# Two quads of heads in one PV bank, K two beats later, second-layer weights turned in beats 1 to 4

## The reference, cut to what matters

```python
x = L0_attn_x                                      # (8, 512, 128) fp32
x = x + attn(layernorm(x))                         # 16 heads of 8
x = x + ffn(layernorm(x))                          # 8 experts, 2 of them for each token

def attn(x):
    Q, K, V = proj(Wq, bq), proj(Wk, bk), proj(Wv, bv)      # (B, 16, 512, 8)
    scores = einsum('bhqd,bhkd->bhqk', Q, K) / sqrt(8)
    attn = softmax(scores)
    out = einsum('bhqk,bhkd->bhqd', attn, V)
    return out.reshape(B, S, D) @ Wo.T + bo

def ffn(t):
    top_v, top_i = top_k(t @ Wr.T + br, 2)                  # router
    h = relu(einsum('bsd,efd->bsef', t, W1) + b1)           # 512 hidden
    o = einsum('bsef,edf->bsed', h, W2) + b2
    return layer_norm(t + sum_over_the_two(o * weight))     # gamma, beta
```

## Time and profile before

| | |
|---|---|
| median of 3 runs | 753.96 us (751.37 to 755.16) |
| profiled execution | 752.29 us, its span 750.5 us |
| busy share of the span | PE 81%, DVE 65%, ACT 60%, POOL 32% |
| scores of T = 0 begin | 33.8 us |
| batches 0 to 7 begin | 33.8, 82.3, 133.6, 193.1, 254.2, 316.1, 377.7, 439.6 us |
| last scores end | 496 us |
| experts' part | about 548 us to the end |

### The profile page before, as it was taken

How to read it: one execution, slowest core, us unless ns; L and a number is a source line. 1 busy time by engine, 2 the same in 40 slices (tenths; PEclk the granted TensorE clock), 3 DMA queues, 4 the chain that set the end, 5 groups by cost and what they waited for, 6 DMA issues and landing times. The chain is left out here.

```text
span 750.5 us, 13269 instructions
## 1 busy us (share of the span) xinstructions
PE 609.3 (81%) x3750; PEld 321.2 (43%) x3750; DVE 489.0 (65%) x1319; ACT 447.4 (60%) x945; POOL 242.6 (32%) x454
## 2 busy tenths in 40 slices
PE   2899999879988997987987998995229998999680
PEld 1633333323333432332332333332128988888530
DVE  3579989968967985985995887751204444444357
ACT  2718888867956965875885786683114444544333
POOL 5200101150240332214115005016425665555534
PEclk9959999989998998998998899899559999999976
DMA  7552122122122122022112211000121221221193
GB/s 219 195 153 66 44 69 83 49 67 74 37 85 72 33 84 84 26 65 89 49 47 70 65 45 48 6 0 30 50 83 54 65 66 56 69 66 57 47 238 98
DMA packets 54216, 54.47 MB, mean 73 GB/s; under 512 B 8286, under 2 KB 37514, under 8 KB 54164
## 3 DMA queue, kind: packets, MB, share of 16 engines
q1 hardware_dynamic: 48372, 44.19, 20.8%
q0 software_dynamic: 4416, 8.53, 3.2%
q10 hardware_dynamic: 1376, 1.13, 0.5%
HBM read 29.01 MB, written 24.81 MB: 72 GB/s over the span
## 5 line engine op out<-in xcount | busy, mean ns | idle before, releaser
L643 DVE TENSOR_REDUCE mneg<-s_psum 128x1 f32<-128x512 f32 x512 | 325.9, 684 | 89.5 <-PE s_psum L810 55.7
L546 ACT ACTIVATE pt<-st_psum 128x512 f32<-128x512 f32 x512 | 279.9, 598 | 93.3 <-PE st_psum L826 82.7
L826 PE MATMUL st_psum<-qs,ks 64*128 64x512 f32 x512 | 202.5, 471 | 24.8 <-ACT pt L546 19.4
L810 PE MATMUL s_psum<-ks,qs 64*128 64x512 f32 x512 | 208.3, 482 | 3.3 <-DVE mneg L643 2.1
L896 PE MATMUL pv_psum<-pt,vst 128*16 128x512 f32 x1024 | 142.8, 632 | 0.0
L810 PEld LDWEIGHTS s_psum<-ks,qs 64*128 64x128 f32 x512 | 84.4, 196 | 120.2 <-DVE mneg L643 94.9
L826 PEld LDWEIGHTS st_psum<-qs,ks 64*128 64x128 f32 x512 | 82.4, 193 | 69.1 <-ACT pt L546 52.7
L1099 ACT ACTIVATE hid<-h_psum,b1c 128x256 f32<-128x256 f32 x144 | 57.2, 474 | 71.2 <-PE h_psum L1204 69.3
L1062 POOL DMA_INDIRECT results<-res,goal_now x72 | 71.6, 994 | 33.7 <-issue 33.7
L1211 PE MATMUL y_psum<-w2t,hid 128*128 128x128 f32 x576 | 73.1, 280 | 0.0
L1211 PEld LDWEIGHTS y_psum<-w2t,hid 128*128 128x128 f32 x576 | 68.9, 194 | 0.9 <-issue 0.2
(11 more groups left out here) (164 smaller groups left out, 711.3 us busy)
## 6 DMA issues: line engine op xcount, KB each, us to landing
parts<-high SPq DMA_DIRECT2D x32, 256.0 KB, 3.0
ks<-parts SPq DMA_DIRECT2D x128, 48.0 KB
qs<-parts SPq DMA_DIRECT2D x128, 48.0 KB
lot<-sent SPq DMA_DIRECT2D x37, 132.0 KB
parts<-low SPq DMA_DIRECT2D x16, 256.0 KB, 3.1
got<-results SPq DMA_DIRECT2D x16, 256.0 KB, 5.1
xres<-in_L_attn_x_dram SPq DMA_DIRECT2D x8, 256.0 KB, 3.6
pt<-in_L_ffn_W_dram SPq DMA_DIRECT2D x1, 2048.0 KB, 14.5
```

The costliest lines, as they stand in the source:

```text
L546: nc.scalar.activation(pt[:, n % PT_SLOTS, (g + 2) % 4, :], st_psum[:, k % ST_BANKS, :], ACT.Exp, scale=SCALE).then_inc(exp_done, 1)
L643: nc.vector.tensor_reduce(mneg[:, (n // 4) % 2, at:at + 1], s_psum[:, k % S_BANKS, :], AX_X, ALU.max, negate=True).then_inc(max_done, 1)
L810: mm(s_psum[:, k % S_BANKS, :], qs[rows, c, P * (n % 4):P * (n % 4) + P], ks[rows, c, g, :], start=True, stop=True).then_inc(s_made, 1)
L826: mm(st_psum[:, k % ST_BANKS, :], ks[rows, c, g, P * (n % 4):P * (n % 4) + P], qs[rows, c, :], start=True, stop=True).then_inc(st_made, 1)
```

## The change

Four edits, in `attention` only.

1. Two quads share the PV bank. Head g of an even quad keeps rows 32g to 32g+15, head g of the odd quad behind it takes rows 32g+16 to 32g+31. A matmul of L896 now has 32 columns of weights instead of 16, of which the 16 of the other quad are zeros, and the bank accumulates over 8 beats. `vst` becomes twice as large. The heads are numbered anew by `head_of`, so that 8 neighbouring heads come out together.
2. The copy of the bank is made in beats 0 and 8, and TURN is in beats 1 and 9; each treats 8 heads. The number of 128x128 transposes, 4 for a TURN, stays.
3. K moves from beat 3 to beat 5 (its store in SP's list with it).
4. The second layer's weights are turned in T = 1 to 4 instead of T = -4 to -1.

```diff
+def per_pair(T, offset):
+    m, r = divmod(T - offset, 8)
+    return m if r == 0 and 0 <= m < QUADS * B // 2 else None
+
+def head_of(c, g):
+    return 8 * (c // 2) + 2 * g + c % 2
...
-    if (q := per_quad(T, 13)) is not None:
-        yield "TURN", q
-    for kind, offset in (("XT", -14), ("K", -13), ("Q", -10), ("V", 7), ("OT", 26), ("O", 27), ("X2T", 30),
+    if (m := per_pair(T, 17)) is not None:
+        yield "TURN", m
+    for kind, offset in (("XT", -14), ("K", -11), ("Q", -10), ("V", 7), ("OT", 26), ("O", 27), ("X2T", 30),
...
 def expert_weights(T):
-    return range(2 * (T + 8), 2 * (T + 8) + 2) if -8 <= T < 0 else ()
+    if -8 <= T < -4:
+        return range(2 * (T + 8), 2 * (T + 8) + 2)
+    return range(E + 2 * (T - 1), E + 2 * (T - 1) + 2) if 1 <= T < 5 else ()
...
-        vst = sb("vst", [P, 2, TILES, H, 16])
+        vst = sb("vst", [P, 2, TILES, H // 2, 64])
...
-                if (b := once(T, -13)) is not None:
+                if (b := once(T, -11)) is not None:
                     store_parts(0, b)
...
-                if (q := per_quad(T, 12)) is not None:
-                    act.wait_ge(pv_made, 4 * q + 4)
+                if (m := per_pair(T, 16)) is not None:
+                    act.wait_ge(pv_made, 8 * m + 8)
...
-                if n % 4 == 0 and q > 0:
-                    pe.wait_ge(pv_copied, q)
+                if n % 8 == 0 and n > 0:
+                    pe.wait_ge(pv_copied, n // 8)
...
                 for g in range(4):
-                    ins = mm(pv_psum[32 * g:32 * g + 16, 0, :], vst[:, b % 2, n % 4, 4 * (q % QUADS) + g, :],
-                             pt[:, n % PT_SLOTS, g, :], start=(n % 4 == 0), stop=(n % 4 == 3))
+                    at = 16 * (q % 2)
+                    ins = mm(pv_psum[32 * g:32 * g + 32, 0, :],
+                             vst[:, b % 2, n % 4, 4 * (q % QUADS // 2) + g, at:at + 32],
+                             pt[:, n % PT_SLOTS, g, :], start=(n % 8 == 0), stop=(n % 8 == 7))
```

More of the change, by code:

```diff
@@ L186, in attention @@
         onorm = sb("onorm", [P, TILES, D])
-        rden = sb("rden", [P, TILES, 4])
+        rden = sb("rden", [P, TILES, 8])
         mneg = sb("mneg", [P, 2, TILES * 4])
@@ L338, in load_parts @@
                     dst = ks[rows, c, g] if w == 0 else qs[rows, c]
-                    sp.dma_start(dst.bitcast(F32), parts[b % 2, w, 4 * c + g]).then_inc(kq_in[c], 16)
+                    sp.dma_start(dst.bitcast(F32), parts[b % 2, w, head_of(c, g)]).then_inc(kq_in[c], 16)
             def beat(T):
@@ L399, in _ @@
             pool.wait_ge(pool_consts, 4)
-            nc.gpsimd.memset(vst[:, :, :, :, HD:HD + 1], 1.0).then_inc(pool_consts, 1)
+            nc.gpsimd.memset(vst[:].rearrange("p z j h (a r) -> p (z j h a) r", r=32)[:, :, HD:HD + 1], 1.0).then_inc(pool_consts, 1)
             nc.gpsimd.memset(tail[:], 0.0).then_inc(tail_ready, 1)
@@ L524, in take_side @@
                         act.wait_ge(pv_made, GROUPS * (of - 1))
-                    nc.scalar.copy(vst[:, of % 2, :, :, 0:HD],
-                                   side_psum[:, 0, :].rearrange("p (j h d) -> p j h d", j=TILES, d=HD))\
+                    nc.scalar.copy(vst[:, of % 2].rearrange("p j h (a r) -> p (j h a) r", r=32)[:, :, 0:HD],
+                                   side_psum[:, 0, :].rearrange("p (x d) -> p x d", d=HD))\
                         .then_inc(side_done, 1)
@@ L532, in beat @@
             def beat(T):
-                if (q := per_quad(T, 12)) is not None:
-                    act.wait_ge(pv_made, 4 * q + 4)
-                    if q >= 1:
-                        act.wait_ge(side_made, SIDE["TURN", q - 1] + 1)
+                if (m := per_pair(T, 16)) is not None:
+                    act.wait_ge(pv_made, 8 * m + 8)
+                    if m >= 1:
+                        act.wait_ge(side_made, SIDE["TURN", m - 1] + 1)
                     nc.scalar.copy(pvs[:], pv_psum[:, 0, :]).then_inc(pv_copied, 1)
@@ L653, in take_early @@
                 elif kind == "TURN":
-                    c = of % QUADS
+                    at = 8 * (of % 2)
                     dve.wait_ge(side_made, SIDE["TURN", of] + 1)
-                    sums = side_psum[:, 0, :].rearrange("p (j g r) -> p j g r", j=TILES, g=4)
+                    sums = side_psum[:, 0, :].rearrange("p (j h r) -> p j h r", j=TILES, h=8)
                     nc.vector.reciprocal(rden[:], sums[:, :, :, HD]).then_inc(rden_done, 1)
@@ L659, in take_early @@
                     nc.vector.tensor_tensor(
-                        onorm[:].rearrange("p j (h d) -> p j h d", d=HD)[:, :, 4 * c:4 * c + 4, :],
-                        sums[:, :, :, 0:HD], rden[:].unsqueeze(3).to_broadcast([P, TILES, 4, HD]),
+                        onorm[:].rearrange("p j (h d) -> p j h d", d=HD)[:, :, at:at + 8, :],
+                        sums[:, :, :, 0:HD], rden[:].unsqueeze(3).to_broadcast([P, TILES, 8, HD]),
                         ALU.mult).then_inc(side_done, 1)
```

## The result

The changed kernel takes 754.94 us (median of 20 executions, 751.17 to 756.77). The kernel before, run beside it, takes 751.88 us (20 executions, 748.38 to 755.19). The ratio is 1.0039, with a 95% interval of 1.0024 to 1.0054: 3 us slower, clear of the noise. Forecast were 741 us and a range of 732 to 750. The profiled execution of the changed kernel took 755.91 us, 754.2 of them in the span.

A forecast was written before the change was run, and what follows sets the result against it. TensorE was taken as nearest to full, DVE close behind, with time lost to stands and slow clock; -4.0 - 1.8 - 6.3 - 1.6 + 1.8 = -11.9 from 752.3 gave 740.4, forecast as 741 us, range 732 to 750.

The forecast's parts named there:

- The start: Second layer's weight transposes leave the way to the first scores: -4.0 us, 2.3 certain and 1.7 chosen, bounds -6.5 and +1.9.
- 1.05 us each at full clock: Ends of T = 1 to 4: eight moved transposes a beat, covered by DVE; at half clock 4.2 us more at worst.
- a fuller TensorE should be slow for less of the 17.1 us: T = 0 to 7: with the moved transposes TensorE would spend less than 17.1 us at 1.2 GHz.
- My lower bound of the gain, +1.9: Start, worst case: 2.3 us gained by the earlier first maximum, 4.2 lost to transposes at half clock.
- Start lost: Rival at the start: moved transposes run at half clock and give back all of the 4.0, 745 us; chance 0.06.
- The change touches neither the scatter nor the work of beats 7 and 8: Beats 7 and 8, where TensorE and DVE stand behind the scatter: left as they are, 0 us.
- scatter stand grows: Rival at beat 8: K's three stores start inside the scatter, 4.2 us more in six scatters, 766 us; chance 0.06.
- TURN of eight heads: Beat 1, where DVE has the router's work: 0.1 us allowed for the longer TURN, inside each -0.35.
- K in beat 5: Beats 3 to 6 take 14.01 us instead of 14.45 at full clock: -0.35 each, five times, -1.8 us.
- The clock behind beat 3: Beats 4 and 5 return to full clock once beat 3's stand is gone: 1.57 us four times, -6.3; bounds 0 and -6.3.
- clock not regained: Rival: beat 3's stand goes, but TensorE still idles and slow stretches fall elsewhere, 747 us; chance 0.20.
- the load's 14 ns: Values with 32 columns: one load's 14 ns more a beat over 128 beats, +1.8 us; bounds 0 and +14.7.

The follow-up runs named there:

- second pair of profiles: The kernel before and the changed kernel run once more, with stands, on another chip: 751.41 us and 754.03 us, ratio 1.0027.
- split start: Changed kernel with four second-layer weight blocks turned ahead of T = 0, four in T = 0 and 1, repeated transposes in T = 2 to 5: 745.23 us, 0.9918.
- filled start: Changed kernel with edit 4 undone and eight unread transposes repeated behind each of beats T = 0 to 5: 747.95 us, 0.9949; the split start also has repeated transposes.
- spread scatter: Kernel before with each scatter's eight transfers issued two a beat in beats 6 to 9: 712.69 us, 1.0003, without stands; three repeats 0.9996, 1.0016, 1.0000.
- the zeros alone: Kernel before with 16 columns of zeros beside the 16 of values, nothing else changed: 711.93 us, 0.9997, and 712.82 us, 1.0002, without stands.

## Why the prediction was wrong

**The start: the step that failed, -4.0 forecast, +6.65 measured (+4.05 in the second pair of profiles).** That the first scores and the first maximum come earlier was right: 4.4 and 3.3 us. Two assumptions behind it were not. The first was that the moved transposes cost "1.05 us each at full clock", with 4.2 us more "at worst". They ran at half clock. T = 1 to 4 take 18.4 us in place of 13.1, each of them above the 3.5 us that I had named as a sign of being wrong. Nor would DVE have covered them wholly at full clock: with the split start, T = 1 takes 2.73 us with eight transposes and was 2.39 before. The second, and the worse one, was that "a fuller TensorE should be slow for less of the 17.1 us". It was slow for 37.5, and T = 5 to 8, which have no moved work, take 18.8 us in place of 13.9. My lower bound of the gain, +1.9, had priced the transposes at half clock and had left all other work at the clock of before; this is why the measurement lies outside it. "Start lost" was the right rival by its mechanism, had a chance of 0.06, and its 745 us were too low for the same reason.

That this edit costs time is shown by the runs without stands: edit 4 alone is slower, 1.0047 (1.0028 to 1.0066), with T = 0 to 7 at 34.09 us. All but edit 4 was 0.9900 and all of it 0.9930, which points the same way, but in two groups and with intervals that overlap. How much longer the half clock lasts by edit 4 is less clear: 27.3 us with edit 4 alone, 17.1 to 27.3 in kernels without it, 37.5 with all four edits in each of three profiles. What in edits 1 to 3 adds the last 10 us beside edit 4 is open; by themselves they have 27.3. Of the +6.65, 2.6 us (6.65 less 4.05) are luck, since the first profile of the kernel before had its short stretch. That it is the clock is shown with stands: filling TensorE's idle time there removed the half clock and made T = 0 to 7 of the kernel without edit 4 23.65 us long, and 23.66 us with half of its transposes in T = 0 and 1. What made the clock fall the rows show only as an order of events. In the changed kernel TensorE stood for 0.79 us, worked for 0.72, stood for 1.66, and the clock was at 1.2 GHz from 31.8 on, at its next matmuls; with edit 4 alone it stood for 2.08 us and fell at 33.4. Before, the 4.20 us of transposes lay directly ahead of the first scores, and it fell at 38.6. I had read these transposes as work in the way of the scores. By the order of the rows they may also be what kept the clock up until there; that is argued and wasn't tried by itself.

On the Trainium skill's rule, "TensorE: Matmul & The Clock Gate", PE-mode transpose, that transposes don't count as busy, I had written that the trace disagrees. The rule's outcome, moved transposes at half clock, is what came. The runs don't bear out the rule as the Trainium skill puts it either: eight transposes behind each beat held 1.00 through T = 0 to 5 once the clock was high, and ahead of the scores, with transposes alone, they had sped up. That the same eight behind beats at 1.2 GHz did not bring it back in T = 1 to 4 would fit the rule. Which property of the work decides is open.

**The scatter: "The change touches neither the scatter nor the work of beats 7 and 8", 0 forecast, +4.9 measured.** With stands, beats 6 to 9 of batches 2 to 7 take 19.46 and 19.43 us on average in the two profiles of the kernel before, and 20.39 and 20.26 in the two of the changed one, of which 0.16 is Q's wait in beat 6. Counted from the start of the scatter, the maxima of beat 8 begin 8.7 to 11.7 us later before, and 11.4 to 11.9 us later in each of the 24 scatters of the changed kernel and of the two with the filled start. So the rival "scatter stand grows" was right in its sign, small in its size (0.8 us a scatter, 0.7 in the second pair, where it needed 2.8 to decide alone), and its reason is not the only one: batch 7 has no K to store and grows most, from 8.7 to 11.6. Edit 4 isn't the cause, since the filled start without it shows 11.6 to 11.8. Which of edits 1 to 3 it is stays open, because the runs that separate them fell in groups without stands. What the stand is stays open too. With it beats 6 to 9 of the changed kernel take 20.3 us on average in batches 2 to 7, without it 12.9, for the same code and the same 9.9 us of scatter on POOL.

**TURN of eight heads: 0.1 allowed, 0.23 measured.** XT in beat 2 and OT in beat 10 wait for it. The timeline of the changed kernel in T = 34:

```profile
146.11 0.35 DVE L670 RECIPROCAL rden<-side_psum 128x32 f32<-128x32 f32 x1
146.50 0.42 DVE L672 TENSOR_TENSOR onorm<-side_psum,rden 128x256 f32<-128x256 f32 x1
147.03 0.42 PEld L869 LDWEIGHTS side_psum<-ident,xn 128*128 128x128 f32 x4 [0.36 <-DVE onorm L672]
```

The groups by line give a mean of 348 ns for the reciprocal and 424 ns for the division, against 248 and 291 before: 0.23 us more in a row, and TensorE's weight load of XT waits 0.36 us for the end of it. The longer beats 2 and 10, 3.25 and 3.22 us for 3.01 and 2.99, are this. I had looked at beat 1, where TURN is issued, and not at beat 2, whose first side task stands behind it, and had forgotten beat 10. It cost 3.1 us, 2.7 in the second pair of profiles; without stands the two beats have the same lengths, 3.25 and 3.22.

**What was right.** K in beat 5: beat 3 without the wait for `low`, 14.0 us for beats 3 to 6. The clock behind beat 3: no drop there in any of the changed kernel's five batches, in any group, while it drops in all five of the group of edit 4 alone (4.71 us for beat 4). So the rival "clock not regained" is out. Beat 13, the load's 14 ns, and copies at nothing were right as well; for the loads +1.8 was taken, and the zeros alone show about 1. My 0.9 ns a column holds only as the price of one more column: it would make 14 ns of a whole load of 16, which takes 95.

**The sum.** Against the profiled execution of before, -11.9 was forecast. The start adds 10.65 to it, the scatter 4.9, beats 2 and 10 add 3.1, and the smaller differences of the table take 3.05 off again: +3.7, the difference of the spans. In the second pair of profiles, with the start of the kernel before at its longer length, the spans differ by 0.8 us.

**A better version.** Edits 1 to 3 with the split and filled start: 0.9918 with stands, and with the spread scatter 0.9811 and 0.9818 without.

## What to carry to other kernels

Work that stands in the way of the critical engine may be what holds its clock (here that is argued, not shown): before moving it, read the granted clock behind the place it leaves, and price everything up to the next change of clock at 1.2 GHz, not only what was moved. When an operation is merged into one twice as large, look for who waits for its end in the beat after it, and count every such beat. A term that rests on the length of a half-clock stretch in one execution needs a second execution, since that length varied between 17.1 and 27.3 us in an unchanged kernel.

## Hardware behaviour that I had not expected

- One and the same kernel has medians of 751 to 752 us in two groups of runs and 712 in four others. Nearly all of it lies in the six batches with a scatter: between two profiles of the changed kernel, with stands and without, 43.9 of 44.4 us, 6.8 to 7.5 in each batch, around beat 8 and the clock behind it.
- 48 extra transposes, 3.4 us less in T = 0 to 7. In the changed kernel TensorE stayed at 1.2 GHz for 37.5 us although it was busy for 36.2 of them; with its gaps filled from T = 0 on it stayed at 2.4 GHz up to the first scatter.
- A load of 32 columns takes 109 ns beside 95 for 16, but eight such loads lengthen a beat by about 8 ns, not by 8 x 14.
